# Adding gated expert outputs into x in DRAM, slot by slot, in a two-layer adaLN kernel

## The reference

```python
h = layernorm(x) * (1 + ca) + sa                  # layer 0
x = x + ga * linear_attention(h)                  # 32 heads x 64, relu q and k
h = layernorm(x) * (1 + cb) + sb
x = x + gb * moe(h)                               # 8 experts of 256, top 2, weights normalised
h = layernorm(x) * (1 + ca) + sa                  # layer 1
x = x + ga * (h + rmsnorm((h @ W_in.T * k) @ W_out.T, norm_w))
h = layernorm(x) * (1 + cb) + sb
x = x + gb * (sparsify_2of4(silu(h @ Wg) * (h @ Wu)) @ Wd)
```

## Time and profile before

| | us |
|---|---|
| median of 3 executions (2035.31, 2037.42, 2040.99) | 2037.42 |
| the profiled execution | 2033.83 |
| its span in the trace | 2032.1 |
| PE busy in the span | 1806.0 (89%) |
| DVE busy | 1231.6 (61%) |
| ACT busy | 718.3 (35%) |
| POOL busy | 658.4 (32%) |

### The profile page before, as it was taken

How to read it: one execution, slowest core, us unless ns; L and a number is a source line. 1 busy time by engine, 2 the same in 40 slices (tenths; PEclk the granted TensorE clock), 3 DMA queues, 4 the chain that set the end, 5 groups by cost and what they waited for, 6 DMA issues and landing times.

```text
span 2032.1 us, 25166 instructions
## 1 busy us (share of the span) xinstructions
PE 1806.0 (89%) x8300; PEld 1425.3 (70%) x8300; DVE 1231.6 (61%) x2094; ACT 718.3 (35%) x1376; POOL 658.4 (32%) x570
## 2 busy tenths in 40 slices
PE   8889999999999999988539999545689999999996
PEld 5557888888888888866437777234578778787785
DVE  4557666666666666687823222688856666656564
ACT  2433544544444544422203343223332222213221
POOL 1436121212121211211340000665745455536342
PEclk9999999999999999998659999867799999999998
DMA  6211343434242424310366663420200111001011
GB/s 233 84 63 59 135 156 134 155 134 155 105 165 89 164 96 186 114 37 6 99 253 243 244 234 137 137 83 16 63 27 13 45 32 47 17 19 52 6 52 42
DMA packets 73150, 209.86 MB, mean 103 GB/s; under 512 B 6204, under 2 KB 6220, under 8 KB 70512
## 3 DMA queue, kind: packets, MB, share of 16 engines
q1 hardware_dynamic: 59184, 153.19, 21.3%
q0 software_dynamic: 6592, 42.04, 5.7%
q10 hardware_dynamic: 7296, 13.63, 2.2%
HBM read 123.05 MB, written 85.79 MB: 103 GB/s over the span
## 4 chain that ended last, share of the span: by engine, by line
PE 64%; DVE 21%; issue 6%; DMA 4%; ACT 2%; POOL 1%; ACTq 0%; DVEq 0%; SPq 0%; POOLq 0%
PE bank L697 20%; PE bank L699 19%; PE bank L698 19%; DMA hs_d<-yt 3%; DVE hh L1946 2%; PE bank L888 2%; PE bank L763 2%; DVE st L1441 1%; DVE rr L1705 1%; DVE tmp L1697 1%; DVE fl L1924 1%; DVE rstd L1425 1%; PE bank L728 1%; DVE na L1423 1%; DVE xw L1493 1%
## 5 line engine op out<-in xcount | busy, mean ns | idle before, releaser
L1705 DVE RECIPROCAL rr<-rr 128x256 f32<-128x256 f32 x128 | 218.8, 1731 | 4.7 <-ACT num L1171 4.7
L697 PE MATMUL bank<-hT,W1b 128*128 128x512 f32 x512 | 210.3, 411 | 12.0 <-DVE hh L1901 11.9
L697 PE MATMUL bank<-W1a,hT 128*128 128x512 f32 x512 | 209.3, 409 | 3.4 <-DVE hT L1619 3.4
L699 PE MATMUL bank<-hT,W1b 128*128 128x512 f32 x512 | 204.3, 399 | 0.0
L698 PE MATMUL bank<-hT,W1b 128*128 128x512 f32 x512 | 203.8, 398 | 0.0
L699 PE MATMUL bank<-W1a,hT 128*128 128x512 f32 x512 | 201.6, 394 | 0.0
L698 PE MATMUL bank<-W1a,hT 128*128 128x512 f32 x512 | 200.9, 392 | 0.0
L2038 POOL TENSOR_TENSOR x<-x,tmp 128x512 f32<-128x512 f32 x64 | 101.2, 1581 | 259.5 <-DVE tmp L1697 259.5
L1724 DVE SCALAR_TENSOR_TENSOR kt<-bank,kt 128x256 fp32r<-128x256 f32 x128 | 50.9, 398 | 173.5 <-ACT vt L1187 173.3
L1901 DVE TENSOR_TENSOR hh<-hh,bank 128x512 f32<-128x512 f32 x64 | 43.2, 686 | 186.2 <-PE bank L699 158.2
L1966 POOL TENSOR_TENSOR W<-stage,W 128x1024 fp32r<-128x1024 f32 x32 | 77.4, 2418 | 189.4 <-ACT W L1079 187.1
(11 more groups left out here) (263 smaller groups left out, 4540.8 us busy)
## 6 DMA issues: line engine op xcount, KB each, us to landing
hs_d<-bor SPq DMA_DIRECT2D x24, 1536.0 KB, 8.6
WB<-ws_d POOLq DMA_DIRECT2D x8, 3072.0 KB
ws_d<-W SPq DMA_DIRECT2D x18, 1024.0 KB, 6.3
stage<-wa SPq DMA_DIRECT2D x32, 512.0 KB, 5.0
stage<-wbe SPq DMA_DIRECT2D x24, 512.0 KB, 3.8
stage<-wdn SPq DMA_DIRECT2D x24, 512.0 KB, 3.8
mw<-wmod SPq DMA_DIRECT2D x10, 1024.0 KB, 4.8
hg<-hs_d SPq DMA_DIRECT2D x39, 256.0 KB, 3.2
```

What stands on the lines that cost most here:

```text
L697: pe.matmul(o, lhs(HI), rhs(HI), start=start, stop=False, **kw)
L699: return pe.matmul(o, lhs(LO), rhs(HI), start=False, stop=stop, **kw)
L1705: dve.reciprocal(rr[:, pair, h], rr[:, pair, h]).then_inc(r_rec, 1)
```

## The change

A row of `hs_d` grows from 512 to 516 values: the first weight, the token's number and its gate row's number, the 512 features, the second weight. The scatter of choice k writes 515 of them, beginning at value k, so that one of the two weights goes along. A new DRAM buffer `u_d` holds x after the attention (behind 128 rows for slots' padding). In each slot DVE takes weight, token number and gate row number out of `hg` into `sm` (`tokens`), POOL gathers 128 gate rows by indirect DMA (`gbt`), DVE reads the down product from PSUM and multiplies it by weight and gate (`weighted`), and POOL adds the 128 rows to `u_d` by an indirect DMA with an addition (`add_out`). Each addition waits until all earlier ones have landed. When the last has landed, SP loads the four batches of x from `u_d`, and `ln_stats` waits for its batch. `gather`, `combine`, ACT's `weighted` and `out_read`, and SP's `rows_store` are gone; the slots' rows are loaded by ACT's queue, the experts' weights by SP's. The core of the diff; the removed functions are printed above:

```diff
+            def begin_sum(b):                         # SP
+                if b == 0:
+                    sp.dma_start(u_d[0:P, :], bor[:, :]).then_inc(ud_stored, 16)
+                sp.wait_ge(ring_done, RING[("tail", "A", GA - 1, b)] + NT)
+                sp.dma_start(u_d[P + b * S:P + (b + 1) * S, :].rearrange("(t p) n -> p t n", p=P),
+                             x[:, b * NT:(b + 1) * NT, :]).then_inc(ud_stored, 16)
             def front():
                 load_x_again(3)
+                begin_sum(2)
                 mrow_load(2)
                 mrow_load(3)
+                load_expert(0)
+                begin_sum(3)
+                load_expert(1)
             def slots():
                 sp.wait_ge(tab_ready, 1)
+                load_expert(2)
+                for i in range(8):
+                    sp.dma_start(mst[:, i, :], winout[i]).then_inc(m_loaded, 16)
+                load_expert(3)
+                wd_slice(0, 0)
+                wd_slice(0, 1)
+                for e in range(4, GE):
+                    load_expert(e)
+            def back():
+                sp.wait_ge(us_done, 16 * SLOTS)
                 for b in range(NB):
+                    sp.dma_start(x[:, b * NT:(b + 1) * NT, :],
+                                 u_d[P + b * S:P + (b + 1) * S, :].rearrange("(t p) n -> p t n", p=P)) \
+                        .then_inc(x_back[b], 16)
...
+                def rows_load(i):                     # ACT, behind silu(i - 4)
+                    if i >= 3:
+                        act.wait_ge(th_full, i - 2)
+                        act.wait_ge(sm_done, i - 2)
+                    at_ = act.value_load(tab[0:1, TAB_ROW, i:i + 1], min_val=0, max_val=HS_ROWS - MT)
+                    act.dma_start(hg[:, i % 3, :], hs_d[bass.ds(at_, MT), :]).then_inc(hg_full[i % 3], 16)
...
-                        dve.wait_ge(x_add, NT * (b + 1))
+                        dve.wait_ge(x_back[b], 16)
...
+                dve.tensor_copy(hb[b][:, :, 1:3].bitcast(I32), idc[:, b * NT:(b + 1) * NT, :])   # front
...
-                dve.tensor_copy(pos[:, :, b * NT:(b + 1) * NT], posf).then_inc(pos_done, 1)
+                dve.tensor_scalar(pos[:, 0, b * NT:(b + 1) * NT], posf[:, 0, :], float(HP), None, ALU.mult)
+                dve.tensor_scalar(pos[:, 1, b * NT:(b + 1) * NT], posf[:, 1, :], float(HP), 1.0, ALU.mult, ALU.add) \
+                    .then_inc(pos_done, 1)
...
+                def tokens(i):                        # DVE
+                    dve.wait_ge(hg_full[i % 3], 16 * (i // 3 + 1))
+                    if i >= 4:
+                        dve.wait_ge(us_done, 16 * (i - 3))
+                    dve.tensor_tensor(sm[:, i % 4, 0:1], hg[:, i % 3, 0:1], hg[:, i % 3, HP - 1:HP], ALU.add)
+                    dve.tensor_tensor(sm[:, i % 4, 1:3].bitcast(I32), hg[:, i % 3, 1:3].bitcast(I32),
+                                      idc[:, NB * NT, :], ALU.max).then_inc(sm_done, 1)
+                def weighted(i):
+                    dve.wait_ge(dn_full, i + 1)
+                    dve.wait_ge(gb_full[i % 2], 16 * (i // 2 + 1))
+                    if i >= 2:
+                        dve.wait_ge(us_done, 16 * (i - 1))
+                    dve.scalar_tensor_tensor(out=yt[:, i % 2, :], in0=bank[6 + i % 2][:, :], scalar=sm[:, i % 4, 0:1],
+                                             in1=gbt[:, i % 2, :], op0=ALU.mult, op1=ALU.mult).then_inc(y_evac, 1)
...
+                def gather_gates(i):                  # POOL
+                    pool.wait_ge(sm_done, i + 1)
+                    if i >= 2:
+                        pool.wait_ge(y_evac, i - 1)
+                    pool.indirect_dma_start(out=gbt[:, i % 2, :], out_offset=None, in_=gates[:, :],
+                                            in_offset=bass.IndirectOffsetOnAxis(
+                                                ap=sm[:, i % 4, 2:3].bitcast(I32), axis=0)).then_inc(gb_full[i % 2], 16)
+                def add_out(i):
+                    pool.wait_ge(y_evac, i + 1)
+                    pool.wait_ge(us_done, 16 * i) if i > 0 else pool.wait_ge(ud_stored, 16 * (NB + 1))
+                    pool.indirect_dma_start(out=u_d[:, :],
+                                            out_offset=bass.IndirectOffsetOnAxis(
+                                                ap=sm[:, i % 4, 1:2].bitcast(I32), axis=0),
+                                            in_=yt[:, i % 2, :], in_offset=None,
+                                            compute_op=ALU.add).then_inc(us_done, 16)
+                gather_gates(0)
+                gather_gates(1)
+                for i in range(SLOTS):
+                    add_out(i)
+                    if i + 2 < SLOTS:
+                        gather_gates(i + 2)
             def back():
-                for b in range(2):
-                    gather(b)
                 for b in range(2):
                     ln_out((2, b), 0)
                     ln_out((2, b), 1)
-                    gather(b + 2)
                     gated_add(b)
```

More of the change, by code:

```diff
@@ L70 @@
 TABW = 40
+HP = H + 4
+ZW = ZERO_ROWS // P * HP // 8
 def split_a_at(g, j):
@@ L297, in over_h1 @@
         def over_h1(a):
[L298 to L305, removed]
+            return a("before_h1", [P, 6144]), a("h1", [P, NT, HP])
+        ((W1a, W2, _, W1b), WB, (_, xw), (_, mw, prow), (_, x0), (_, h1)) = shared(
+            [weights, lambda a: a("WB", [P, 2, 2, 3072], F32R), over_w2, over_mods, over_x0, over_h1])
+        hold2 = sb("hold2", [P, 12304])
         def over_pro(a):
@@ L464, in build @@
         dn_full = sem("b_down_full")
[L465 to L471, removed]
+        y_evac = sem("b_slot_out_weighted")
+        id_ready = sem("token_numbers_ready")
+        ud_stored = sem("b_sum_begun")
+        sm_done = sem("b_slot_tokens_copied")
+        gb_full = [sem(f"b_slot_gates_gathered{i}") for i in range(2)]
+        us_done = sem("b_slot_out_added")
+        x_back = [sem(f"b_x_loaded{b}") for b in range(NB)]
         m_loaded = sem("m_loaded")
@@ L1294, in slots @@
                 act_hi(SLOTS - 1)
-                out_read(SLOTS - 1)
-            def weighted(b):
-                for t in range(NT):
-                    act.wait_ge(yg_full[b % 2][t], 32 * (b // 2 + 1))
-                    act.activation(yg[b % 2][:, t, 0, :], yg[b % 2][:, t, 0, :], ACT.Copy,
-                                   scale=wk[:, 0, b * NT + t:b * NT + t + 1]).then_inc(x_u0, 1)
             def back():
-                load_row("B", 0, 0)
-                load_row("B", 0, 1)
                 crows(0, 0)
                 crows(1, 0)
-                weighted(0)
                 for half, banks in ((0, (0, 1)), (1, (4, 5))):
@@ L1314, in back @@
                 ln_out((2, 0), 1)
-                weighted(1)
                 crows(0, 1)
@@ L1481, in apply_rows @@
                     dve.wait_ge(ln_chain, chain["ln"])
-                    last = dve.scalar_tensor_tensor(out=hb[b][:, t, :], in0=hb[b][:, t, :], scalar=rstd[:, t:t + 1],
+                    last = dve.scalar_tensor_tensor(out=xn_of(1, b)[:, t, :], in0=xn_of(1, b)[:, t, :], scalar=rstd[:, t:t + 1],
                                                     in1=mrow[:, 1, :], op0=ALU.mult, op1=ALU.add)
@@ L1832, in slots @@
                         rows_lo(i + 1)
+                        tokens(i + 1)
                     product(i)
+                    if i >= 1:
+                        weighted(i - 1)
                 act_lo(SLOTS - 1)
-            def combine(b):
-                for t in range(NT):
-                    n = b * NT + t
-                    dve.wait_ge(x_u0, n + 1)
-                    dve.scalar_tensor_tensor(out=yg[b % 2][:, t, 0, :], in0=yg[b % 2][:, t, 1, :],
-                                             scalar=wk[:, 1, n:n + 1], in1=yg[b % 2][:, t, 0, :], op0=ALU.mult,
-                                             op1=ALU.add).then_inc(x_u1, 1)
-                dve.wait_ge(row_full[b % 2], ROW_LOADS["B"] + 16 * (b // 2 + 1))
-                for t in range(NT):
-                    n = b * NT + t
-                    dve.wait_ge(x_u1, n + 1)
-                    dve.tensor_tensor(yg[b % 2][:, t, 0, :], yg[b % 2][:, t, 0, :], row[:, b % 2, :],
-                                      ALU.mult).then_inc(x_g, 1)
-                for t in range(NT):
-                    n = b * NT + t
-                    dve.wait_ge(x_g, n + 1)
-                    dve.tensor_tensor(x[:, n, :], x[:, n, :], yg[b % 2][:, t, 0, :], ALU.add).then_inc(x_add, 1)
+                weighted(SLOTS - 1)
             def back():
-                combine(0)
                 stats((2, 0), range(NT))
@@ L1865, in back @@
                 gated(0)
-                combine(1)
                 stats((2, 1), range(NT))
@@ L1871, in step_c @@
             def step_c(b):
-                if b < 2:
-                    combine(b + 2)
                 ln = layernorms("C", 0, b)
@@ L2118, in scatter @@
                 pool.wait_ge(xn_ready, ln_index(1, b) + 1)
```

(1 more changed line is left out.)

159 lines of the change are left out of this document (59 added, 100 removed).

## The result

The changed kernel is slower: 2076.01 us median of four executions (2070.9 to 2079.18) beside 2037.15 for the kernel before on the same chip, a ratio of 1.0186 (95% interval 1.0161 to 1.0211), about +38 us. The forecast was 1997.

What follows compares the result with a forecast made beforehand. PE was taken to bound the slots and DVE the stretch behind them; front -4, slots 0 and back -36 make -40, from 2033.83 to 1993.8, plus 3.6 for the runs' median: 1997 us, range 1985 to 2040.

Steps and rivals of the forecast that it cites:

- the back: Behind the slots, M and layer 1's mixing: waits and combine work on DVE's path go, -36 us (bounds -29 and -45).
- PE's wait behind M: After M, PE's 4.29 us wait for DVE's xn returns, less 1 for ACT's split of M: -3.3 us.
- DVE's two stalls of 5: Behind the slots, DVE's 5.58 and 5.32 us in operations on four values: -5 us (bounds 0 and -10).
- the front: Ahead of the slots: first rows land in 3.2 instead of 8.45, +1 for added DVE work: -4 us (-6 to +2).
- the chain of additions: In the slots: each addition waits for the previous landing, repeating every 3.7 us, below the slots' 4.81, so no loss.
- P: Period of the serial additions in the slots: wake-up 0.3 plus landing 3.4 us, 3.7 together.
- the loads: Slots with an expert load: additions land after 10 to 12 us, stalls stay about 2.2: 0 us (-13 to +13).
- The one that made the kernel slower: In the slots, additions set the pace wholly: period 6.66 us, +57 there, +17 overall, 2054 us; chance 0.18.
- the other one: In the slots, additions set the pace in part: period 5.7 us, +20, 2017 us; chance 0.15.

Runs made afterwards that it cites:

- two sums: Changed kernel, even and odd slots adding into two DRAM buffers, each addition waiting for the one two slots before, second buffer not added to x: 2033.45 us.
- four buffers: Two sums kernel with four buffers of yt and gbt and eight of sm, instead of two and four: 2009.63 us, slots 219.6.
- the pieces: Changed kernel with each expert's 3 MB loaded in 12 DMAs of 256 KB, packets of 2 KB instead of 24 KB: 2068.07 us.
- both ways of pacing the load: Kernel before, third to eighth expert's weights in 12 pieces of 256 KB, two or four under way: 2099.63 and 2054.65 us.

## Why the prediction was wrong

**Right: the back.** -35.8 for a forecast of -36. PE's wait behind M went (-4.3, forecast -3.3), `combine` left DVE's path, and DVE's two stalls of 5 are gone; given back are 2.1 at each of two L1495, which run beside `gated_add`. That it fits to a fraction of a us is luck: with the same back the other runs took 161.8 to 164.5 for a stretch of 163.4. **Right in kind: the front.** The first rows land in 2.65, but the last scatter starts 3.7 later (1052.74 for 1049.05), where I had set +1: -2 for -4.

**Wrong: the chain of additions.** The step that failed reads "with one more such phase the landing is 2.73 + 0.68 = 3.4, and P = 3.7. I take that". Measured were a landing of 4.7 to 5.5, inside my bounds of 2.73 and 6.36, and 0.77 until the next issue instead of 0.3, so P = 5.5 to 6.1, on the wrong side of the slots' 4.85. Against the scatters ahead of the slots (2.73 and 2.93) an addition costs 2 to 2.5 us more, over three times the data phase of 0.68 that I added, and 0.6 of it is POOL's issue (1.58 for 0.96). Against the 4.0 that a scatter took in the slots it costs some 1.2 more, so the scatter's own price was too low there as well. That the chain costs 36 of the 71 us is shown from two sides, by plain scatters (277.6 to 241.1) and by two sums (241.5).

**Wrong: the loads.** "Two `yt` buffers and four of `sm` give it a little under two slots [...], so a stall stays about what it is". An addition beside a load does land after about 11 to 13, where I had 10 to 12, but the room is not what the store had: `tokens` and `weighted` wait ahead of DVE's low parts, the gates' gather is ordered only some 1.5 slots ahead and is as late, and a chain that is over pace by itself never catches up. With two sums the intervals at the loads are still 10.5 to 12.4, some 6 to 7.5 over the pace, where the kernel before lost 2.2 at each. Of the 241.5 - 206.7 = 35 us left after the chain, four buffers return 22, and the rest went only when the additions went (199.2). Part of a stall's price is PE's clock behind it, which no term of the sum had: with two sums PE was busy 14 us longer than before for the same matmuls. The mechanism that I gave for the late landing, packet by packet, fell with the pieces; what does make a transfer late beside a load stays open.

**The rivals.** The one that made the kernel slower named the place (DVE behind `tokens` and `weighted`, then PE) and forecast 2054, but with a period of 6.66 that was not reached. The measured 5.5 to 6.1 is the period of the other one, where the additions set the pace in part (5.7, so 2017). The loads brought the rest, which both left at nothing; that the first of the two has the right sign is in part luck.

**Open.** Where the last stage's 3.9 us go. Why an addition needs more than a scatter, and a scatter more in the slots than ahead of them: both are measured, not explained.

## What to carry to other kernels

Before a chain of DMAs that wait for each other goes into a pipelined loop, price its period as landing plus the waiting queue's way to the next issue, and take an unmeasured DMA at its upper bound when the lower and the upper bound lie on both sides of the loop's pace. Where a bulk load shares the DMA engines, count how many slots each small transfer may be late before an in-order engine waits for it; two more buffers were worth 13 us here in the old kernel, where both ways of pacing the load made it slower. Writing each row once to a place of its own and adding later, partly under PE's work, beat adding in DRAM (2004.14 with four buffers, where the additions with four took 2063.77).

## What the runs showed of the hardware

Away from the loads an indirect DMA of 128 rows of 2 KB with an addition took 4.7 to 5.5 us from issue to landing, where the plain one took 2.73 and 2.93 ahead of the slots and about 4.0 in them, and 1.58 instead of 0.96 on POOL to issue. An expert's 3 MB in twelve DMAs of 256 KB, all queued at once, delayed the other queues nearly as much as one DMA of 3 MB: the intervals at loads were 11 to 12 us instead of 12 to 15. With two under way a piece of 256 KB needed 3.9 to 4.6 us in the median of a run, and the 3 MB 24 to 30. Behind a wait of 5.07 us PE's matmuls started 0.42 to 0.43 us apart instead of 0.23 for some 4 us.
